# Four ends of stages in a two-layer graph kernel: products, row turns, first loads and batch statistics placed elsewhere

## The chip, the cores and the metric

The kernel runs on one NeuronCore of a Trainium2 chip. The metric is the device time of one execution in microseconds (us). The engines are PE (TensorE; PEld is its weight load), DVE (VectorE), ACT (ScalarE), POOL (GpSimd, which issues the gathers) and SP (SyncE, which issues the other DMAs).

## The reference, cut to what matters

```python
x = layernorm(x + L0(x))          # L0: GCN, two gcn_conv (128 -> 256 -> relu -> 128)
x = layernorm(x + L1(x))          # L1: attention messages, GRU, batch norm
# gcn_conv: h = x @ W; agg = segment_sum(h[src] * norm, dst) + h * dinv**2 + b
# L1, with 50000 nodes and 25000 edges sorted by dst:
att = sigmoid(xs @ W_att[:d] + xd @ W_att[d:] + b_att)        # xs = x[src], xd = x[dst]
aggregated = segment_sum((xs @ W_msg + b_msg) * att, dst)
gi = aggregated @ W_ih.T + b_ih;  gh = x @ W_hh.T + b_hh
r = sigmoid(i_r + h_r);  z = sigmoid(i_z + h_z);  n = tanh(i_n + r * h_n)
h_new = (1 - z) * n + z * x
return gamma * (h_new - mean(h_new, 0)) * rsqrt(var(h_new, 0) + eps) + beta
```

## The kernel before

The 50000 nodes are cut into NG = 98 groups of 512. After a preparation the kernel runs five passes over the groups, `scale`, `conv`, `norm`, `gru` and `final`. Each engine has its own program; in each pass it runs a function of the pass's name once per step, and `group_of(lag)` in it is the group that entered `lag` steps ago, so a step works on several groups, each at another phase. `run_pass` writes the first and the last steps out and makes loops of the rest. For `norm` the loops are unrolled by 8. Every order on an engine is that in which the code is written. Semaphores named by pass (`a_` conv, `n_` norm, `c_` gru, `o_` final) count finished groups.

The input may be irregular; a flag `slow_i`, worked out at the start, says so. PE, DVE and ACT have a FAST and a SLOW version of the passes with gathers, in two `If` blocks behind each other; the input here takes FAST. `both_ways` writes the two blocks. POOL issues three indirect gathers for each group in `conv`, `norm` and `gru` (`gathers`, L695), into four buffers `gath`.

- **conv** makes `G` (the rows that `norm` gathers, written by SP at L568) and `OWN` (the rows' own part, L570). Both DMAs of a group count on the same semaphore `a_st`. POOL starts `norm`'s gathers once all of `a_st` is in (`conv_rows_stored`).
- **norm**, on PE: the group's sum from the gathered rows (L1396, lag 0), its transposition (L1404, lag 4), the recurrent product of the candidate gate, `whh_sb[:, 2D:3D]` times the turned rows (L1410, lag 6), and the two attention columns (L1413, lag 6). DVE adds `OWN` (L1141, lag 2), makes the one-hot tiles (L1145, lag 0), copies the attention columns (L1153, L1154, lag 8; they release SP's store of `MT`, L589), and takes the row statistics (L1167 and the small ones after, lag 2 and 3). ACT takes the root (L810), scales (L816, lag 3), moves the turned rows out (L824, lag 5) and the recurrent product (L830, lag 7).
- **Between norm and gru**: outside the `If`, PE turns the collected attention columns `AD_ALL` (4 transpositions, L1420), ACT moves the result to `n_r[0]` (L835), SP stores it as `AD` (four DMAs, L597), and waits for all stores (`general_clear`). POOL starts gathering `MT` as soon as the stores of `YT` and `MT` are in.
- **gru**: SP loads for each group a row of `AD` to all partitions (`c_ad`, L611), at lag 2 the turned rows `YT` (`c_y`, L617) and, for 44 groups, `HN` (L620). The load of the attention row of groups 1, 2, 3 waits until ACT has finished the attention sigmoid (L868, `c_sgs`) of the group before it. DVE makes weighted one-hots (L1208), PE sums (L1445, lag 1) and, at lag 3, makes five products of 128x512: L1431 and L1437 from `whh_sb` and `c_y` for the gates r and z, L1433, L1435 and L1438 from the sum. On ACT L847 to L876 are the gates and a square with its sum over nodes; on DVE L1217 to L1237.
- **Behind gru**, outside the `If`: DVE reduces the sums (L1244 to L1249), ACT takes one root (L886, which needs another activation table, a load of its own at the same line), DVE makes factor and offset (L1251 to L1254), and **final** begins: POOL applies them (L741), PE transposes (L1465), DVE and ACT do the second row norm.

```python
            both_ways(norm, 6, unroll=8)          # PE, before
            pe.wait_ge(n_mc, NG)
            pe.wait_ge(n_trc, NG)
            for q, rows in enumerate(AD_CHUNKS):
                last = nc.tensor.transpose(bank[3][0:rows, q * P:(q + 1) * P], AD_ALL[:, q * P:q * P + rows], ident[:])
            last.then_inc(n_adt, 1)
            pe.wait_ge(n_hk, NG)
```

## Time and profile before

| | |
|---|---|
| median of 3 runs | 1756.09 us (1754.35 to 1758.73) |
| the profiled execution | 1759.59 us |
| its span in the trace | 1757.5 us |
| busy share of the span | PE 84%, DVE 80%, ACT 68%, POOL 60% |
| DMA moved | 433.97 MB, mean 247 GB/s |

The span runs from the first to the last instruction. The passes stand in it at about 189 to 626 us (conv), 631 to 1034 us (norm), 1045 to 1569 us (gru) and 1569 to 1757 us (final). Between two passes there is a seam in which most engines stand still: they can be seen in the page as low digits of PE's row.

### The profile page before, as it was taken

How to read it: one execution, taken by the hardware profiler on the slowest of the kernel's cores; microseconds unless marked ns; L12 is line 12 of the kernel's file. 1: busy time of each engine (PE TensorE's matmuls, PEld its weight loads, DVE VectorE, ACT ScalarE, POOL GpSimd, SP SyncE). 2: the span in 40 equal slices, each digit the busy share in tenths (PEclk: the TensorE clock that was granted, in tenths of full speed). 3: DMA queues.
4: the chain of work that ended last, by engine and by line, in shares of the span. 5: the costliest groups of instructions: out<-in, count | busy, mean ns of one | idle time of the engine just before them, and what ended most of it. 6: DMA issues, size and time to landing. Idle time of an engine off the chain costs nothing.

```text
span 1757.5 us, 35422 instructions
## 1 busy us (share of the span) xinstructions
PE 1473.8 (84%) x7678; PEld 1042.8 (59%) x7678; DVE 1398.1 (80%) x4668; ACT 1196.8 (68%) x3010; POOL 1053.4 (60%) x1014
## 2 busy tenths in 40 slices
PE   6300699999999958899999959999999999976765
PEld 3200477777777747778787845555555555545554
DVE  7817699999999858888888826888888888877786
ACT  6786355555555527777776746777777777757898
POOL 5000677777777547777777735666666666614442
PEclk9755799999999979999999979999999999988898
DMA  8798799998888738898776747777754444439998
GB/s 262 264 342 308 241 328 331 329 317 271 270 269 270 262 118 274 298 313 300 250 235 224 242 152 222 233 226 232 228 167 130 127 128 127 132 99 384 374 324 277
DMA packets 246942, 433.97 MB, mean 247 GB/s; under 512 B 41831, under 2 KB 44108, under 8 KB 246848
## 3 DMA queue, kind: packets, MB, share of 16 engines
q1 hardware_dynamic: 218160, 393.40, 65.8%
q0 software_dynamic: 28688, 39.54, 9.4%
q8 instruction: 31, 0.51, 0.1%
q14 instruction: 63, 0.52, 0.1%
HBM read 274.13 MB, written 178.01 MB: 257 GB/s over the span
## 4 chain that ended last, share of the span: by engine, by line
PE 61%; POOL 11%; DMA 11%; issue 6%; DVE 6%; ACT 4%; SPq 1%; DVEq 0%; ACTq 0%; POOLq 0%
POOL gath L695 10%; PE bank L1379 10%; PE bank L1371 10%; PE bank L1363 5%; PE bank L1431 5%; PE bank L1433 5%; PE bank L1445 5%; PE bank L1435 5%; PE bank L1438 5%; PE bank L1437 5%; DMA page<-YT 3%; PE bank L1396 3%; DMA gath<-G,ROWI 3%; ACT page L901 2%; DMA page<-in_x 2%
## 5 line engine op out<-in xcount | busy, mean ns | idle before, releaser
L695 POOL DMA_INDIRECT gath<-MT,ROWI x294 | 325.1, 1106 | 199.7 <-PE bank L1445 115.6
L695 POOL DMA_INDIRECT gath<-XP,ROWI x294 | 332.1, 1130 | 171.7 <-issue 88.7
L695 POOL DMA_INDIRECT gath<-G,ROWI x294 | 294.4, 1001 | 116.9 <-issue 83.8
L791 ACT ACTIVATE page<-bank,b_sb 128x512 f32<-128x512 f32 x196 | 124.0, 684 | 152.7 <-PE bank L1371 152.7
L1379 PEld LDWEIGHTS bank<-w_sb,page 128*128 128x128 f32 x1568 | 190.3, 192 | 46.4 <-issue 46.4
L1396 PE MATMUL bank<-gath,onehot 128*128 128x128 f32 x1176 | 161.0, 288 | 47.3 <-DMA gath<-G,ROWI 44.7
L1379 PE MATMUL bank<-w_sb,page 128*128 128x128 f32 x1568 | 190.7, 275 | 0.0
L1371 PE MATMUL bank<-page,w_sb 128*128 128x512 f32 x392 | 185.8, 597 | 0.0
L1363 PE MATMUL bank<-onehot,gath 128*128 128x170 f32 (+1 forms) x588 | 104.1, 314 | 94.9 <-DMA gath<-XP,ROWI 94.9
L1396 PEld LDWEIGHTS bank<-gath,onehot 128*128 128x128 f32 x1176 | 144.3, 198 | 51.2 <-issue 39.0
L1465 PE MATMUL bank<-ident,page 128*128 128x128 f32 x784 | 119.0, 304 | 62.2 <-DMA page<-YT 57.2
L816 ACT ACTIVATE page<-page,st_m,st_r 128x128 f32<-128x128 f32 x392 | 160.1, 479 | 0.0
L901 ACT ACTIVATE page<-bank,p_m,p_r 128x128 f32<-128x128 f32 x392 | 144.3, 497 | 22.2 <-DVE p_m L1287 13.1
L799 ACT ACTIVATE page<-bank,DINV 128x128 f32<-128x128 f32 x392 | 111.7, 368 | 58.5 <-PE bank L1379 57.9
L1465 PEld LDWEIGHTS bank<-ident,page 128*128 128x128 f32 x784 | 96.6, 155 | 85.2 <-issue 45.3
L1363 PEld LDWEIGHTS bank<-onehot,gath 128*128 128x128 f32 x588 | 88.9, 195 | 96.9 <-issue 94.5
L1413 PEld LDWEIGHTS bank<-watt_sb,page 128*128 128x128 f32 x784 | 103.6, 192 | 47.8 <-issue 47.3
L1445 PEld LDWEIGHTS bank<-onehot,gath 128*128 128x128 f32 x588 | 95.6, 193 | 59.7 <-issue 45.9
L861 ACT ACTIVATE page<-bank,brz_sb 128x512 f32<-128x512 f32 x98 | 67.3, 687 | 80.6 <-PE bank L1433 80.6
L1208 DVE SCALAR_TENSOR_TENSOR onehot<-iota_b,LOC,page 128x170 f32<-128x170 f32 (+1 forms) x294 | 98.9, 391 | 22.8 <-ACT page L868 22.5
L1120 DVE SCALAR_TENSOR_TENSOR page<-page,DINV 128x128 f32<-128x128 f32 x392 | 110.6, 341 | 5.9 <-issue 5.9
L868 ACT ACTIVATE page<-page,gath 128x170 f32<-128x170 f32 (+1 forms) x294 | 106.0, 426 | 13.3 <-DMA page<-AD 13.3
(224 smaller groups left out, 3292.7 us busy)
## 6 DMA issues: line engine op xcount, KB each, us to landing
page<-YT SPq DMA_DIRECT2D x196, 256.0 KB, 3.4
MT<-page SPq DMA_DIRECT2D x98, 260.0 KB, 3.3
XP<-page SPq DMA_DIRECT2D x98, 256.0 KB, 2.5
page<-in_xT SPq DMA_DIRECT2D x98, 256.0 KB
page<-DQ SPq DMA_DIRECT2D x98, 256.0 KB
G<-page SPq DMA_DIRECT2D x98, 256.0 KB
OWN<-page SPq DMA_DIRECT2D x98, 256.0 KB
page<-OWN SPq DMA_DIRECT2D x98, 256.0 KB
```

The lines of the kernel that those rows point to most:

```text
L695: nc.gpsimd.indirect_dma_start(gath[k][:, w, 0:width], None, rows, bass.IndirectOffsetOnAxis(ap=ROWI[:, at:at + 1], axis=0), bounds_check= ...
L791: last = nc.scalar.activation(rows[k], bank[2 + 2 * k + h][:], ACT.Relu, bias=b1_sb[:, h:h + 1])
L799: last = nc.scalar.activation(a_g[k][:, own], bank[6 + g.slot(2)][:, own], ACT.Copy, scale=DINV[:, bass.ds(g.index * J + j, 1)])
L816: last = nc.scalar.activation(n_m[g.slot(8)][:, j * DM:j * DM + D], n_z[k][:, j * D:(j + 1) * D], ACT.Identity, bias=st_m[k][:, j:j + 1], ...
L901: last = nc.scalar.activation(o_o[k][:, j * D:(j + 1) * D], bank[g.slot(8)][:, j * D:(j + 1) * D], ACT.Identity, bias=p_m[g.slot(8) // 2][ ...
L1120: last = nc.vector.scalar_tensor_tensor(a_r[k][:, own], a_g[k][:, own], DINV[:, bass.ds(g.index * J + j, 1)], a_xb[k][:, own], ALU.mult, A ...
L1363: last = nc.tensor.matmul(bank[k][:, at:at + n], gath[g.slot(4)][:, w, 0:D], onehot[k][:, at:at + n], start=True, stop=True)
L1371: last = nc.tensor.matmul(bank[2 + 2 * k + h][:], w1_sb[:, h * P:(h + 1) * P], a_T[k], start=True, stop=True)
L1379: last = nc.tensor.matmul(bank[6 + k][:, j * D:(j + 1) * D], rows[k][:, j * P:(j + 1) * P], w2_sb[:, h, :], start=(h == 0), stop=(h == 1))
L1396: last = nc.tensor.matmul(bank[k][:, j * D:(j + 1) * D], onehot[k][:, first:first + P], gath[g.slot(4)][:, w, 0:D], start=(i == 0), stop=( ...
L1445: last = nc.tensor.matmul(bank[k][:, at:at + n], gath[g.slot(4)][:, w, 0:D], onehot[k][:, at:at + n], start=True, stop=True)
L1465: last = nc.tensor.matmul(out_bank[:, tile], part[k][:, tile], ident[:], is_transpose=True, start=part is o_y and j == 0, stop=part is o_t ...
```

## The change

1. **Stores of conv**: the stores of `OWN` count on semaphores of their own (`own_st`, later used for the loads of `norm`). POOL waits for the stores of `G` alone before the first gather of `norm`. ACT and DVE wait, inside conv, each for its own kind.
2. **End of norm, PE**: the recurrent products of the last four groups (94 to 97) are taken out of the pass. Behind the last attention columns, still inside the `If`, PE makes those of groups 94 and 95, then the four transpositions of `AD_ALL`, then those of 96 and 97. ACT moves them out at matching places.
3. **norm, DVE**: the copy of the attention columns goes from lag 8 to lag 7, and from ahead of the row statistics to the end of the step. This holds in every step.
4. **Start of gru**: SP loads `c_y` of groups 0 and 1 ahead of the first attention row. PE makes their four products from `whh_sb` (r and z) before the first sum.
5. **End of gru**: the batch statistics on DVE and the root on ACT stand inside the `If` (in both versions), and ACT calls a root of a constant first, which brings its table in.

```diff
@@ gathers of norm, POOL
             def conv_rows_stored():
-                wait_all_dmas(pool, a_st, 2)
+                wait_all_dmas(pool, a_st)
                 pool.wait_ge(a_agg, NG)
@@ conv, SP
-                    sp.dma_start(group_of_table(OWN, g), a_r[k]).then_inc(a_st[k], 16)
+                    sp.dma_start(group_of_table(OWN, g), a_r[k]).then_inc(own_st[k], 16)
@@ gru, SP
+            for k in range(2):
+                sp.dma_start(c_y[k], YT[k:k + 1].rearrange("a p n -> (a p) n")).then_inc(c_iny[k], 16)
...
-                    sp.dma_start(c_y[k], group_of_table(YT, g)).then_inc(c_iny[k], 16)
+                    if not (g.fixed and g.index < 2):
+                        sp.dma_start(c_y[k], group_of_table(YT, g)).then_inc(c_iny[k], 16)
@@ norm, ACT
-            run_pass(act, norm, 7, unroll=8)
+            run_pass(act, norm, 6, unroll=8)
+            late = [Group(index // 8, index % 8, unroll=8) for index in range(LATE, NG)]
+            for g in late[:2]:
+                hidden(g)
             act.wait_ge(n_zz, NG)
             act.wait_ge(n_adt, 1)
             nc.scalar.activation(n_r[0], bank[3][:], ACT.Copy).then_inc(n_ad, 1)
+            for g in late[2:]:
+                hidden(g)
@@ gru, ACT
+            def batch_root():
+                nc.scalar.activation(p_q[0][:, 0:1], eps_sb[:, 0:1], ACT.Sqrt)
+                act.wait_ge(bn_v, 1)
+                nc.scalar.activation(bn[:, 3:4], bn[:, 2:3], ACT.Sqrt, bias=eps_sb[:, 1:2]).then_inc(bn_r, 1)
...
             with act.If(flag < 1):
                 run_pass(act, lambda group_of: gru(group_of, FAST), 5)
+                batch_root()
@@ norm, DVE
-                if g := group_of(8):
-                    k = g.slot(4)
...
+                normaliser(group_of(2), group_of(3), n_s6, n_sd, n_root, n_dq, n_var, n_rs)
+                if g := group_of(7):
...
-            both_ways(norm, 8, unroll=8)
+            both_ways(norm, 7, unroll=8)
@@ norm, PE
-                    wait(pe, n_hk, g.freed(2))
-                    nc.tensor.matmul(bank[6 + g.slot(2)][:], whh_sb[:, 2 * D:3 * D], y, start=True, stop=True).then_inc(n_hn, 1)
+                    if not (g.fixed and g.index >= LATE):
+                        recurrent(g)
...
+            def norm_end():
+                late = [Group(index // 8, index % 8, unroll=8) for index in range(LATE, NG)]
+                pe.wait_ge(n_trc, NG)
+                for g in late[:2]:
+                    recurrent(g)
+                pe.wait_ge(n_mc, NG)
+                for q, rows in enumerate(AD_CHUNKS):
+                    last = nc.tensor.transpose(bank[3][0:rows, q * P:(q + 1) * P], AD_ALL[:, q * P:q * P + rows], ident[:])
+                last.then_inc(n_adt, 1)
+                for g in late[2:]:
+                    recurrent(g)
@@ gru, PE
+                if g and g.fixed and g.index == 0 and mode is FAST:
+                    pe.wait_ge(n_ad, 1)
+                    for k in range(2):
+                        pe.wait_ge(c_iny[k], 16)
+                        nc.tensor.matmul(bank_r[k][:], whh_sb[:, 0:D], c_y[k], start=True, stop=False)
+                        nc.tensor.matmul(bank_z[k][:], whh_sb[:, D:2 * D], c_y[k], start=True, stop=False)
```

At the end of `norm` PE's row of instructions was this (before; `ident,DSQ` are the transpositions of the collected columns, `page,whh_sb` a recurrent product, `watt_sb,page` attention columns):

```order
L1404 MATMUL bank<-ident,page 128x128 x4
L1410 MATMUL bank<-page,whh_sb 128x512
L1413 MATMUL bank<-watt_sb,page 128x2 x4
L1410 MATMUL bank<-page,whh_sb 128x512
L1413 MATMUL bank<-watt_sb,page 128x2 x4
L1410 MATMUL bank<-page,whh_sb 128x512
L1413 MATMUL bank<-watt_sb,page 128x2 x4
L1351 UNCONDITIONAL_BRANCH
```

And now, in the lines of the changed file (L1445 transposes a group, L1426 is the recurrent product, L1454 the attention columns, L1464 turns the collected ones):

```order
L1445 MATMUL bank<-ident,page 128x128 x4
L1454 MATMUL bank<-watt_sb,page 128x2 x12
L1426 MATMUL bank<-page,whh_sb 128x512 x2
L1464 MATMUL bank<-ident,DSQ 128x128 x3
L1464 MATMUL bank<-ident,DSQ 8x128
L1426 MATMUL bank<-page,whh_sb 128x512 x2
L1386 UNCONDITIONAL_BRANCH
L1389 COMPARE_AND_BRANCH
```

The products went behind the columns, and the turning came inside the branch.

One step of `norm` on DVE, last written-out step ahead of the loop, before:

```order
L1141 TENSOR_TENSOR page<-bank,page 128x512
L1145 TENSOR_SCALAR onehot<-iota_b,LOC,WD 128x256 x3
L1153 COPY DSQ<-bank 128x4
L1154 TENSOR_TENSOR page<-bank,batt_sb 128x4x2
L1167 BN_STATS st<-page 128x6 x4
L1176 RECIPROCAL st_r<-st_q 128x4
```

and now (L1193 is the row statistics, L1184 and L1185 copy the attention columns):

```order
L1168 TENSOR_TENSOR page<-bank,page 128x512
L1172 TENSOR_SCALAR onehot<-iota_b,LOC,WD 128x256 x3
L1193 BN_STATS st<-page 128x6 x4
L1202 RECIPROCAL st_r<-st_q 128x4
L1203 SCALAR_TENSOR_TENSOR st_m<-st_s,st_q 128x4
L1208 TENSOR_TENSOR st_d<-st 128x4
L1209 TENSOR_TENSOR st_s<-st 128x4
L1210 TENSOR_TENSOR st_v<-st 128x4
L1212 TENSOR_TENSOR st_d<-st_d 128x4
L1216 TENSOR_TENSOR st_m<-st_m,st_r 128x4
L1220 SCALAR_TENSOR_TENSOR st_v<-st_d,st_v 128x4
L1184 COPY DSQ<-bank 128x4
```

The copy, which waits for PE's attention columns, is now the last thing of a step and stands ahead of the next step's addition.

The start of `gru` on PE, before (L1445 is the sum, L1431 and L1437 the products from `whh_sb`):

```order
L1445 MATMUL bank<-onehot,gath 128x172
L1445 MATMUL bank<-onehot,gath 128x170 x2
L1431 MATMUL bank<-page,whh_sb 128x512
L1433 MATMUL bank<-page,wc_sb 128x512
L1435 MATMUL bank<-page,wc_sb 128x512
L1437 MATMUL bank<-page,whh_sb 128x512
L1438 MATMUL bank<-page,wc_sb 128x512
```

and now (L1479 and L1480 are the four early products, L1503 the sum, L1490, L1492 and L1496 the rest of a group):

```order
L1479 MATMUL bank<-page,whh_sb 128x512
L1480 MATMUL bank<-page,whh_sb 128x512
L1479 MATMUL bank<-page,whh_sb 128x512
L1480 MATMUL bank<-page,whh_sb 128x512
L1503 MATMUL bank<-onehot,gath 128x172
L1503 MATMUL bank<-onehot,gath 128x170 x2
L1503 MATMUL bank<-onehot,gath 128x172
L1503 MATMUL bank<-onehot,gath 128x170 x2
L1490 MATMUL bank<-page,wc_sb 128x512
L1492 MATMUL bank<-page,wc_sb 128x512
L1496 MATMUL bank<-page,wc_sb 128x512
```

Two products of each of the first two groups now stand ahead of every sum.

## Rows read from the trace of the kernel before

**Rows 1.** Busy time by stretch: PE, PEld, DVE, ACT, POOL, then PEclk, DMA share, GB/s

```profile
700.00:760.00 60.00, 55.02 (x403) 47.48 (x403) 51.48 (x282) 43.49 (x108) 45.93 (x47) 1.00 0.92 307
940.00:1000.00 60.00, 57.29 (x398) 49.01 (x398) 50.17 (x271) 42.20 (x106) 45.99 (x47) 0.94 0.70 228
1180.00:1240.00 60.00, 60.00 (x185) 31.90 (x184) 50.63 (x106) 47.10 (x105) 38.80 (x36) 1.00 0.74 231
```

**Rows 2.** Chain that ended last, seam between conv and norm: start us, us, what

```profile
626.61 3.83 DMA OWN<-page
630.46 0.74 issue
631.20 0.99 POOL gath L695
```

**Rows 3.** Timeline there, SP's queue: start us, us, engine line op out<-in [idle before <-releaser]

```profile
625.38 0.33 SPq L568 DMA_DIRECT2D G<-page  x1
```

**Rows 4.** Timeline inside norm, one step of DVE and PE

```profile
902.70 0.69 DVE L1141 TENSOR_TENSOR page<-bank,page 128x512 f32<-128x512 f32 x1
...
903.55 0.95 PE L1413 MATMUL bank<-watt_sb,page 128*128 128x2 f32 x8
...
904.65 0.16 DVE L1153 COPY DSQ<-bank 128x4 f32 x1 [0.26 <-PE bank L1413]
...
906.32 0.69 DVE L1141 TENSOR_TENSOR page<-bank,page 128x512 f32<-128x512 f32 x1
```

**Rows 5.** Timeline, last steps of norm, DVE and ACT

```profile
1021.32 0.16 DVE L1153 COPY DSQ<-bank 128x4 f32<-128x4 f32 x1 [1.25 <-PE bank L1413]
...
1025.68 1.64 ACT L816 ACTIVATE page<-page,st_m,st_r 128x128 f32<-128x128 f32 x4
```

**Rows 6.** Chain that ended last, from norm's last products to gru's first load

```profile
1032.06 0.96 PE bank L1410 x2
1033.02 0.80 PE bank L1413 x8
...
1034.09 1.85 issue
1035.94 0.87 PE bank L1420 x3
1036.82 2.37 issue
...
1044.89 3.30 DMA page<-AD
```

**Rows 7.** Timeline, first steps of gru, ACT and PE

```profile
1048.21 1.09 ACT L868 ACTIVATE page<-page,gath 128x172 f32<-128x172 f32 x3 [6.44 <-DMA page<-AD]
...
1052.53 1.09 ACT L868 ACTIVATE page<-page,gath 128x172 f32<-128x172 f32 x3 [3.22 <-DMA page<-AD]
...
1058.30 2.07 PE L1431 MATMUL bank<-page,whh_sb 128*128 128x512 f32 x2 [1.51 <-DMA page<-YT]
...
1063.03 1.09 ACT L868 ACTIVATE page<-page,gath 128x172 f32<-128x172 f32 x3 [0.23 <-DMA page<-AD]
...
1075.14 1.03 PE L1445 MATMUL bank<-onehot,gath 128*128 128x172 f32 x6
```

**Rows 8.** One line's DMAs (L617, `page<-YT`), 1040 to 1075 us: landing

```profile
DMA to landing us min/median/max: 2.8/4.7/5.9
```

**Rows 9.** Timeline, end of gru, ACT and DVE

```profile
1569.13 0.19 ACT L876 ACTIVATION_READ_ACCUMULATOR page<-keep 128x1 f32 x1
...
1570.98 0.26 DVE L1244 TENSOR_REDUCE bn<-hsum 128x1 f32<-128x98 f32 x1 [2.28 <-issue]
...
1571.36 1.28 ACT L886 ACT_TABLE_LOAD   x1 [2.04 <-issue]
```

**Rows 10.** Timeline, end of norm, ACT's earlier change of table, and the copy ahead of it

```profile
1039.66 0.60 ACT L835 ACTIVATE page<-bank 128x512 f32<-128x512 f32 x1 [6.00 <-PE bank L1420]
1040.28 1.28 ACT L836 ACT_TABLE_LOAD   x1
```

More of the change, by code:

```diff
@@ L52 @@
 BACK = max(at - P * w for w, (at, n) in enumerate(FAST_COLS))
+LATE = NG - 4
 AD_CHUNKS = [min(P, NT - at) for at in range(0, NT, P)]
@@ L1255, in _ @@
+            flag = dve.value_load(slow_i[0:1, 0:1], min_val=0, max_val=1)
+            chained = count[0]
+            with dve.If(flag < 1):
+                run_pass(dve, lambda group_of: gru(group_of, FAST), 4)
+                batch_map()
+            count[0] = chained
+            with dve.If(flag > 0):
+                run_pass(dve, lambda group_of: gru(group_of, SLOW), 4)
+                batch_map()
             wait_all_dmas(dve, h_st, 2, FREE)
@@ L1346, in _, with both_ways @@
             general_tensor(pe, 0, D)
-            def both_ways(step, lag, unroll=U):
+            def both_ways(step, lag, unroll=U, end=lambda: None):
                 flag = pe.value_load(slow_i[0:1, 0:1], min_val=0, max_val=1)
@@ L1385, in _, with recurrent @@
             general_tensor(pe, 1, D)
+            def recurrent(g):
+                wait(pe, n_hk, g.freed(2))
+                nc.tensor.matmul(bank[6 + g.slot(2)][:], whh_sb[:, 2 * D:3 * D], n_T[g.slot(4)], start=True, stop=True).then_inc(n_hn, 1)
             def norm(group_of, mode):
@@ L1414, in norm @@
                     last.then_inc(n_mm, 1)
-            both_ways(norm, 6, unroll=8)
-            pe.wait_ge(n_mc, NG)
-            pe.wait_ge(n_trc, NG)
-            for q, rows in enumerate(AD_CHUNKS):
-                last = nc.tensor.transpose(bank[3][0:rows, q * P:(q + 1) * P], AD_ALL[:, q * P:q * P + rows], ident[:])
-            last.then_inc(n_adt, 1)
+            def norm_end():
[9 more added lines that the diff above has]
+                    recurrent(g)
+            both_ways(norm, 6, unroll=8, end=norm_end)
             pe.wait_ge(n_hk, NG)
```

83 lines of the change are left out of this document (48 added, 35 removed).

## The prediction

> **What bounds the kernel now.** I read the busy time by stretch first, then the chain of work that ended last, then the timeline at each seam. In `norm` POOL is the bound: 46 or 47 gathers in 60 us, 45.93 to 45.99 us busy, and each gather is followed by 0.30 us of its own issue, so that 46 of them fill the 60 us at 1.30 each [rows 1]. A group costs 3 x 1.30 = 3.9 us. PE has 55 to 57 of 60 us there and DVE 50 to 51, so both keep slack, PE little. In `gru` PE is busy 60.00 of 60 us: it is the bound, and a group takes 5.16 us (16 matmuls a group, 185 in 60 us) [rows 1]. What is won inside these passes on DVE, ACT or SP is worth nothing; what is won at a seam moves the whole rest. So I price the seams, and ask of every edit inside a pass whether it could make a new bound.
>
> **Seam conv to norm.** POOL's first gather at 631.20 follows the landing of the last store of `OWN`, issued at 626.61 and landed 3.83 us later [rows 2]. The last store of `G` was issued at 625.38 [rows 3]. With the same landing time it is in 1.23 us earlier, and the 0.74 us of issue behind it stays. POOL is the bound up to the last gather, so this passes on to the end of the pass: **-1.2 us**. It can't be below 0, since the new wait is a part of the old one, and little above. ACT, DVE and SP now wait for eight semaphores rather than four; this is hidden, since the first one-hot is needed only when three gathers have landed, some 5 us after the first. Inside conv the split waits free nobody: the chain runs through PE there.
>
> **Norm on DVE.** The copy L1153 waits for PE's attention columns. In a steady step the next addition L1141 started at 902.70, before PE's columns of that step (903.55 to 904.50), and DVE waited 0.26 us for them at 904.65; the next step began at 906.32 [rows 4]. So DVE works 3.62 - 0.26 = 3.36 us in a step. Now the columns come first: the addition starts about 2 us later against PE. Behind the waiting copy are queued the addition (0.7 us), on which PE's sum two steps on waits, and the one-hots (1.1 us). PE's sum needs them one PE step later, which is 3.5 us, and they are there after 0.2 + 0.7 + 1.1 = 2.0. DVE's own 3.36 stays under 3.9. Price in the steady part 0; there POOL's buffers cover it (four groups deep). The bound on the other side is a rival below.
>
> **End of norm.** Here PE is the chain. In the last steps a group costs one recurrent product of 0.96 and columns of 0.80 us [rows 6]. Taking out the four products removes 3 x 0.96 = 2.9 us from the path; the fourth (group 94) I count at nothing, because PE would then wait for the last transposition, which needs ACT's scaling at 1025.68 [rows 5]. The moved copy costs a bit: DVE's copy at 1021.32, which had waited 1.25 us, now stands ahead of the addition of group 97, which had run during that wait, so that statistics come 0.7 us later [rows 5]. Most of this fits into slack on ACT; I count +0.2. Sum so far -2.7.
>
> From the end of the last columns (1033.82) to the end of the turning (just ahead of ACT's copy at 1039.66 [rows 10]) the chain had 5.8 us: DVE's copy, 1.85 us of issue, three transpositions 0.87, 2.37 of issue, the fourth [rows 6]. Now two products come first, 2 x 0.96 = 1.9, and cover DVE's copy; then four transpositions in straight code, 0.87 + 0.4, and 0.1 for semaphores: 3.3. That is -2.5, and the term **-5.2 us**. Between ends: if the 2.37 returns at some point of the new piece, -2.8; if all goes smoother, -5.9. The two remaining products lie behind the turning and beside ACT's copy and SP's stores. `MT`'s last store goes 2.7 us earlier, so the gathers do as well; they were not last before.
>
> The two idle times of 1.85 and 2.37 us in which PE waited for nothing shown stand right behind the end of the `If` [rows 6]; I take them to be the cost of leaving it. The Trainium skill, Runtime: NRT & Kernel Launch, Instruction fetch mechanics, says that a taken branch whose target is not at hand makes the engine fetch by DMA first, and that straight code is fetched ahead. By that rule PE still pays behind its last products, where SP's stores (over 5 us to the next load at 1044.89) cover it.
>
> **Start of gru.** Count from S, SP's first load (1044.89). Before: first attention sigmoid at S+3.3, the second at S+7.6, the fourth at S+18.1, PE's first product only at S+13.4, at half clock (two matmuls in 2.07 us), and the fifth sum at S+30.3 (1075.14); from there PE runs without a gap [rows 7]. The attention rows climb a ladder, since each load waits for the sigmoid before: 14.8 us for three rungs. Now two `YT` loads stand ahead of the first row. Two issues cost about 0.8 us; and a row lands in 3.3 us alone [rows 6], while loads in a crowd took 2.8 to 5.9, median 4.7 [rows 8]. I take 4.3, nearer the crowd's median: the first sigmoid at S+5.1, 1.8 later than before (between 0.7 and 3.4). The rungs lose two `YT` loads as company; I take 4.75 each, between the quickest rung of 4.32 and the mean of 4.94 [rows 7]: the fourth sigmoid at S+19.4. The four early products (3.4 us at full clock, 8.3 at 2.07 each) run from about S+4; the first sum may be late by 2 to 3 us, but the second waits for the second rung anyway. Behind the ladder PE no longer has ten products for two groups to make up but six, so it keeps pace, and what is late next is the ladder plus one round of ACT and DVE: 1.1 for the sigmoid, 2.2 for ACT's other gates (4.1 us a group less sigmoid and square), 4.4 for DVE's group [rows 1]. The fifth sum comes at 19.4 + 1.1 + 2.2 + 4.4 = S+27.1 instead of S+30.3: **-3.1 us** (from -1.5 to -4.2 by the delay of the first row; 0 if PE is late too).
>
> **End of gru.** ACT's last square ended at 1569.32; DVE's first reduction came at 1570.98, ACT's table load at 1571.36 after 2.04 us of idle time, and the root behind it at 1572.64 [rows 9]. Now the load starts at 1569.35 and ends at 1570.63, the root of the constant takes 0.2, and DVE's reductions, 1.2 us from 1569.4, are done by then: root at 1570.9. **-1.8 us**. The way out of the `If` now lies behind the factor, where ACT and DVE wait for PE's first turned rows. The final pass has to load its table again (1.28), hidden in the same wait.
>
> A table load took 1.28 us and began 0.02 us after an activation [rows 10]. The Trainium skill, ScalarE: Activation LUTs, What ACT_TABLE_LOAD costs, adds a drain of some 1380 ns to every switch. That would be a result of its own: the last term would shrink to -0.4 and the time rise by 1.4. The row speaks against it, and I go by the row.
>
> **Sum.** 1.2 + 5.2 + 3.1 + 1.8 = 11.3 us. Against the profiled execution 1759.59 this is 1748.3. That execution lay 3.5 us above the median of the runs shown (1756.09), so I forecast 1744.8. The lows of the terms, 0 + 2.8 + 0 + 0.4, give 3.2 (1752.9); the highs, 1.3 + 5.9 + 4.2 + 1.9, give 13.3 (1742.8), and two medians of runs may differ by 2 us.
>
> **Rivals.**
> - *The front of gru gives nothing*: attention rows behind two loads of 256 KB, or the early products at half clock in the way of the first sums. For: rows 8 allow a delay of 3.4. Against: PE has nothing else to do until the first attention sigmoid, over 8 us behind its last transposition [rows 7, 10]. Sum 8.2, 1747.9. Chance 0.13.
> - *The issue gap returns* in the new end of norm (1747.2), alone 0.08, together with the rival above (1750.3) 0.06; *the drain is real* (1746.2) 0.03.
> - *The seams don't add up*: the gains don't pass on, because DMA-bound stretches (92% in norm's first half [rows 1]) or the final pass take them back; 1753 or so, 0.07.
> - *Slower*: the copy at the end of a DVE step ties DVE to PE. If waits for the columns, the addition and PE's sum closed a loop longer than POOL's 3.9 us, each 0.1 us would cost 9.6 us over some 96 groups. It decides against us from 4.02 us on; at 4.1 the time is 1744.8 + 19 = 1764. For: PE has only 3 to 5 us of slack in 60. Against: the 1.5 us of room worked out above, and buffers four deep. 0.05.
> - *Forecast*: 0.58.
>
> **Chances.** A measurement can tell about 0.3% from no change, so faster means below 1750.8. Faster 0.82, within 0.3% 0.13, slower 0.05. Range for 8 in 10: 1740.5 to 1753.
>
> **What would show it.** The first gather of norm about 1.2 us nearer the last sum of conv; gathers still 1.30 us apart through norm; no idle time above 0.5 us between PE's last columns and the end of the turning; the first attention sigmoid 5 us behind SP's first load of gru, and the fifth sum at 27; the table load directly behind the last square. It is wrong if PE waits for DVE inside norm, if a gap of 2 us stands between the transpositions, or if the fifth sum still comes 30 us behind the first load.

## The result

The changed kernel took 1754.61 us, median of 12 runs, beside 1759.15 us for the kernel before in the same comparison: a ratio of 0.9976 with a 95% interval of 0.9965 to 0.9986. The forecast was 1744.8, with a range up to 1753.0, so the measured time lies outside it. The difference is 4.5 us where 11.3 were forecast. Some 3 us of the miss in the absolute time come from the three runs of before that the forecast started from (1756.09); the rest is a gain that isn't there. The ratios leave out slow executions, here one of the changed kernel (2337.71 us at a mean granted clock of 0.64) and two of the kernel before (1910.51 and 2346.03 us). Three later comparisons of the same two kernels gave 0.9986, 0.9984 and 0.9979, so that the four together stand at 0.998, or some 3.4 us. The sign was right; by the bound of 0.3% the change makes no difference.

The profiled execution has a span of 1752.3 us, against 1757.5 before. In the seam between conv and norm the chain of work that ended last (start us, us, what) now follows the last store of `G`:

```profile
626.40 4.14 DMA G<-page
630.54 0.03 POOLq L728
630.57 0.74 issue
631.31 1.00 POOL gath L705
```

From that store's issue to the first gather 4.91 us went by, where 5.82 had (625.38 to 631.20, [rows 2, 3]). The last sum of norm then started at 1017.5 us here and 1017.6 before, since the last store of `G` itself had gone out 1.0 us later (626.40 against 625.38). The same chain at the end of norm reads quite unlike [rows 6]:

```profile
1028.58 1.09 PE bank L1445 x4
1029.67 4.91 PE bank L1454 x24
1034.58 3.62 PE bank L1426 x4
1038.20 0.74 PE bank L1464 x4
```

The 24 matmuls of three groups' attention columns (L1454) took 4.91 us, 1.64 a group, where a group's had taken 0.80. Two recurrent products (L1426, four matmuls) took 3.62, 1.81 each, where they had taken 0.96. The turning itself (L1464) has lost both idle times of 1.85 and 2.37 us. The reason for the slow products is in PE's windows (from:to, length, PE busy and count, granted clock, DMA share, GB/s):

```profile
1026.00:1028.00 2.00, 1.42 (x12) 1.00 0.65 250
1028.00:1030.00 2.00, 1.42 (x8) 0.60 0.43 159
1030.00:1034.00 4.00, 4.00 (x20) 0.50 0.87 330
1034.00:1038.00 4.00, 4.00 (x8) 0.50 0.36 135
```

The granted clock fell from 1.00 (2.4 GHz) to 0.50 (1.2 GHz) within the second of two pieces in which PE was busy 1.42 of 2 us. Most of the idle time in them is one wait of 1.09 us, until ACT had moved turned rows out (L835), where before PE had a recurrent product to do:

```profile
1028.58 1.09 PE L1445 MATMUL bank<-ident,page 128*128 128x128 f32 x4 [1.09 <-ACT page L835]
```

In the kernel before, the same rows of windows read:

```profile
1030.00:1032.00 2.00, 1.87 (x15) 1.00 0.43 162
1032.00:1034.00 2.00, 2.00 (x12) 1.00 1.02 383
1034.00:1036.00 2.00, 2.00 (x13) 1.00 0.94 355
```

(These are from a second profile of before, in which everything from norm on lies some 3 us later; it is the kernel e12 below.)

At the start of gru, PE's timeline (start us, us, engine, line, operation, [idle before <-releaser]) shows the early products L1479 and L1480 behind the two loads, and the fifth sum at 1072.21 instead of 1075.14 [rows 7]:

```profile
1048.09 2.04 PE L1479 MATMUL bank<-page,whh_sb 128*128 128x512 f32 x2 [7.45 <-DMA page<-YT]
1049.93 1.91 PE L1480 MATMUL bank<-page,whh_sb 128*128 128x512 f32 x2
...
1056.31 1.14 PE L1503 MATMUL bank<-onehot,gath 128*128 128x172 f32 x6 [1.58 <-DVE onehot L1234]
...
1072.21 1.11 PE L1503 MATMUL bank<-onehot,gath 128*128 128x172 f32 x6 [0.27 <-issue]
```

At the end of gru the chain no longer passes through the batch factor. It goes from ACT's last square to SP and to a load of the final pass:

```profile
1565.88 0.58 ACT page L896 x2
1566.46 0.02 issue
...
1566.55 0.33 SPq L646
...
1567.87 4.98 DMA page<-YT
```

### The profile page after: what moved, and what is told of

The parts are those of the page before. It is cut to its first block, busy times and chain, and to the rows that moved or that the text cites. A ratio compares the mean times of both kernels' runs of the same rounds, so it can differ in the third digit from the quotient of the medians.

```text
span 1752.3 us, 35433 instructions
## 1 busy us (share of the span) xinstructions
PE 1476.5 (84%) x7678; PEld 1042.4 (59%) x7678; DVE 1394.2 (80%) x4668; ACT 1197.3 (68%) x3012; POOL 1057.6 (60%) x1014
## 4 chain that ended last, share of the span: by engine, by line
PE 56%; POOL 16%; DMA 10%; issue 7%; ACT 4%; DVE 4%; SPq 1%; DVEq 0%; ACTq 0%; POOLq 0%
POOL gath L705 16%; PE bank L1416 10%; PE bank L1408 9%; PE bank L1503 5%; PE bank L1490 5%; PE bank L1488 5%; PE bank L1496 5%; PE bank L1492 5%; PE bank L1495 5%; PE bank L1400 5%; DMA page<-YT 3%; ACT page L927 2%; DMA page<-in_x 2%; DMA XP<-page 1%; PE bank L1523 1%
## 5 line engine op out<-in xcount | busy, mean ns | idle before, releaser
L705 POOL DMA_INDIRECT gath<-XP,ROWI x294 | 336.1, 1143 | 172.8 <-issue 84.1
L1437 PE MATMUL bank<-gath,onehot 128*128 128x128 f32 x1176 | 161.0, 288 | 45.0 <-DMA gath<-G,ROWI 43.4
L1437 PEld LDWEIGHTS bank<-gath,onehot 128*128 128x128 f32 x1176 | 144.0, 197 | 49.4 <-issue 34.6
L1454 PEld LDWEIGHTS bank<-watt_sb,page 128*128 128x128 f32 x784 | 105.8, 197 | 46.0 <-issue 46.0
L1503 PEld LDWEIGHTS bank<-onehot,gath 128*128 128x128 f32 x588 | 93.9, 190 | 52.3 <-issue 48.4
L821 ACT ACTIVATE st_q<-st_v,eps_sb 128x4 f32<-128x4 f32 x98 | 29.1, 297 | 130.6 <-DVE st_v L1220 128.9
```

The lines of the kernel that those rows point to most:

```text
L705: nc.gpsimd.indirect_dma_start(gath[k][:, w, 0:width], None, rows, bass.IndirectOffsetOnAxis(ap=ROWI[:, at:at + 1], axis=0), bounds_check= ...
L1437: last = nc.tensor.matmul(bank[k][:, j * D:(j + 1) * D], onehot[k][:, first:first + P], gath[g.slot(4)][:, w, 0:D], start=(i == 0), stop=( ...
L1503: last = nc.tensor.matmul(bank[k][:, at:at + n], gath[g.slot(4)][:, w, 0:D], onehot[k][:, at:at + n], start=True, stop=True)
```

## The experiments

**How they are compared.** From each profile I read the same marks: the start of norm's last sum, the end of the attention columns, the end of the turning, and the start of gru's fifth sum, from which PE is busy without a longer gap. The table gives them in us after the last sum's start, by the timelines, and the ratio of times to the kernel before with its interval. (By the chain the sum starts 0.13 us later; the expectations of the first runs count the changed kernel's 21.41 from there, as 21.28.) "Late" is the number of recurrent products taken out of the pass; "order" is the place of DVE's attention copies (old: lag 8, ahead of the statistics; new: lag 7, behind them).

| kernel | late | order | turning in branch | columns | turning | fifth sum | ratio |
|---|---|---|---|---|---|---|---|
| before | 0 | old | no | 16.20 | 21.95 | 57.53 | |
| e12 (before again) | 0 | old | no | 16.20 | 21.95 | 57.52 | |
| e16 seam only * | 0 | old | no | 16.20 | 22.14 | 58.17 | 0.9993 (0.9984 to 1.0002) |
| e8 batch statistics only * | 0 | old | no | 17.30 | 22.77 | 59.71 | 0.9996 (0.9982 to 1.0009) |
| e11 late only | 4 | old | no | 16.33 | 20.75 | 56.61 | 0.9982 (0.9972 to 0.9991) |
| e9 turning only | 0 | old | yes | 16.21 | 17.19 | 54.73 | 0.9981 (0.9969 to 0.9994) |
| changed kernel | 4 | new | yes | 17.06 | 21.41 | 54.69 | 0.9976 (0.9965 to 0.9986) |
| e6 (changed again) * | 4 | new | yes | 15.80 | 19.85 | 52.77 | 0.9986 (0.9972 to 1.0000) |
| e13 (changed again) * | 4 | new | yes | 15.93 | 20.04 | 53.88 | 0.9984 (0.9974 to 0.9994) |
| e18 (changed again) * | 4 | new | yes | 16.83 | 21.30 | 55.42 | 0.9979 (0.9966 to 0.9992) |
| e2 old order | 4 | old | yes | 13.97 | 18.45 | 50.53 | |
| e14 (e2 again, timed) * | 4 | old | yes | 17.24 | 21.55 | 55.54 | 0.9973 (0.9962 to 0.9984) |
| e4 changed, with filler | 4 | new | yes | 14.25 | 17.59 | 51.48 | 0.9956 (0.9939 to 0.9973) |
| e1 no late | 0 | new | yes | 16.92 | 17.97 | 51.73 | 0.9941 (0.9926 to 0.9956) |
| e10 no late, old order | 0 | old | yes | 16.20 | 17.24 | 50.60 | 0.9954 (0.9937 to 0.9970) |
| e17 (e10 again) * | 0 | old | yes | 17.14 | 18.19 | 54.68 | 0.9966 (0.9953 to 0.9979) |
| e3 two late | 2 | new | yes | 15.21 | 16.25 | 49.06 | 0.9939 (0.9925 to 0.9952) |
| e15 (e3 again) * | 2 | new | yes | 15.41 | 16.46 | 52.75 | 0.9972 (0.9962 to 0.9982) |
| e5 two late, old order * | 2 | old | yes | 15.72 | 17.23 | 52.52 | 0.9958 (0.9941 to 0.9974) |
| e7 as e5, no gru front * | 2 | old | yes | 15.33 | 16.84 | 54.87 | 0.9960 (0.9944 to 0.9976) |

The rows with a star ran on three other chips (e5 to e8, e13 to e16, e17 and e18), on which the kernel before takes 1852 to 1865 us instead of 1759 to 1761. Norm takes 452 to 462 us there from first gather to last sum, and 386 to 388 elsewhere. Times are compared with the kernel before on the same chip only.

**e1, no late product.**

```
-LATE = NG - 4
+LATE = NG
-            run_pass(act, norm, 6, unroll=8)
+            run_pass(act, norm, 7, unroll=8)
```

> The changed kernel with the four last recurrent products back in the pass; the turning of the attention rows stays inside the branch, and the rest of the change stays. Theory A: taking the products out of the drain leaves TensorE idle, its granted clock falls to half, and the attention columns then cost 1.64 us a group instead of 0.79. Then here the granted clock stays at 1.00 to the end of the columns; last sum's start to the end of the columns 16.1 to 16.7 us (changed kernel 16.92, before 16.07), turning done 1.3 to 2.5 us later, so 17.6 to 18.8 in all against 21.28 and 21.83: a span 2.5 to 3.7 us shorter than the changed kernel's, 1748.6 to 1749.8. Theory B (the two vector copies, issued ahead of the statistics, make the last groups late and TensorE idle for them): the clock still falls near the end, 20 to 21.3 us in all, span 1751 to 1752.5. Theory C (the products do cost their 0.96 us each, and the fall of the clock belongs to the end of the stage whatever is issued): 21.3 us or more, span at least 1752.

Measured: 17.97 us to the end of the turning, a ratio of 0.9941, span 1750.2 (0.4 above what theory A had given it; the columns ended 0.1 us later than it had). The clock was at 1.00 to the end of the columns. All four products are back in PE's way, and the stretch is 3.4 us shorter than in the changed kernel's first profile. PE's timeline shows columns at 0.8 us a group to the end, and the turning 0.42 us behind them:

```profile
1033.81 1.10 PE L1426 MATMUL bank<-page,whh_sb 128*128 128x512 f32 x2
1034.75 0.95 PE L1454 MATMUL bank<-watt_sb,page 128*128 128x2 f32 x8
1036.12 0.63 PE L1464 MATMUL bank<-ident,DSQ 128*128 128x128 f32 x4 [0.42 <-DVE page L1185]
```

**e2, the old vector order, four late.** The two copies stand ahead of the statistics again, as at lines 1149 to 1154 of the kernel before.

> The changed kernel with VectorE's pair of attention copies back behind the statistics' place of before (lag 8, ahead of them); the four products stay late. Theory A: TensorE still idles in the drain where the products stood, the granted clock still falls to half, and last sum's start to the end of the turning stays within 0.7 us of the changed kernel's 21.28 us. Theory B: the statistics of the last group start 0.65 us earlier, the two idle stretches of 0.67 and 1.14 us before the last sums go, the clock stays at 1.00, and the same stretch takes 16.5 to 17.5 us. Theory C: as A.

Measured, in one execution of 1753.82 us beside 1760.09: 18.45 us, with the clock at half from 13 us after the last sum on. Most of the columns had run at the full clock by then, and they ended at 13.97. The stretch is 3 us shorter than the changed kernel's, which spoke for theory B in part. It was timed again later (e14), and that took it back.

**e3, two late products, both behind the turning.**

```
-LATE = NG - 4
+LATE = NG - 2
-                for g in late[:2]:
+                for g in late[:0]:
...
-                for g in late[2:]:
+                for g in late:
```

> The changed kernel with only the last two recurrent products taken out of the pass, and both put behind the turning. Theory A: the products of groups 94 and 95 keep TensorE at work, as far as they stand between the last sums the clock stays at 1.00 (or falls late, after most of the columns); last sum's start to the end of the turning 15.2 to 17 us against 21.28: a span 4 to 6 us shorter than the changed kernel's, 1746.3 to 1748.3, the fastest of these. Theory B: the last groups are late as before, the clock falls with them, 20 to 21.3 us, span 1751 to 1752.3. Theory C: only the products' place counts, 19.4 to 21.3 us, span 1750.4 to 1752.3.

Measured: 16.25 us, the shortest of all, and a ratio of 0.9939. The clock stayed at 1.00 until behind the turning; three groups' columns took 2.59 us in the chain, as against 4.91. The profiled span, 1753.2, is above the 1746.3 to 1748.3 expected; it belongs to the slowest of its five executions (1755.29; the others lie at 1748.3 to 1751.2), and the excess lies in the final pass.

**e4, more work.** The changed kernel with one product that nobody reads, ahead of each of the last two groups' transpositions:

```
+                    if g.fixed and g.index >= NG - 2:
+                        wait(pe, n_zz, NG - 1)
+                        nc.tensor.matmul(bank[0][:], whh_sb[:, 2 * D:3 * D], keep[:, 0:GN], start=True, stop=True)
                     wait(pe, n_yy, g.done())
```

> The changed kernel with work added: TensorE multiplies whh_sb by 512 columns of keep into bank 0, once ahead of each of the last two groups' transpositions, and nothing reads the result (the outputs stay what they were). Each costs about one product, 0.96 us at the full clock. Theory A: more work, less time: TensorE stays busy where it idled, the granted clock stays at 1.00 into the columns, and last sum's start to the end of the turning falls below the changed kernel's 21.28 us, to 16.5 to 19. Theories B and C: the added products cost 0 to 1.9 us, 21.3 to 23.2 us, span 1752.3 to 1754.2.

Measured: 17.59 us, ratio 0.9956. PE's timeline shows the fillers (L1444) and behind them three groups' columns (L1457) in 2.74 us, and its windows the full clock under them:

```profile
1029.62 1.10 PE L1444 MATMUL bank<-keep,whh_sb 128*128 128x512 f32 x2
1030.67 0.63 PE L1448 MATMUL bank<-ident,page 128*128 128x128 f32 x4
1031.13 2.74 PE L1457 MATMUL bank<-watt_sb,page 128*128 128x2 f32 x24
1033.73 2.62 PE L1426 MATMUL bank<-page,whh_sb 128*128 128x512 f32 x4
1036.15 1.06 PE L1467 MATMUL bank<-ident,DSQ 128*128 128x128 f32 x4
```

```profile
1030.00:1032.00 2.00, 2.00 (x15) 1.00 0.43 160
1032.00:1034.00 2.00, 2.00 (x18) 1.00 1.02 384
```

Work was added, the order of everything else was kept, and the stretch became 2.3 to 3.8 us shorter than in the four profiles of the changed kernel (19.85 to 21.41). The rivals allowed no gain from it. The idle time of 1.1 us is gone with it. This is the experiment on which theory A rests.

**e6, the changed kernel again, and e5, both causes out.** e5 is e3 with DVE's old order.

> The changed kernel once more, as the yardstick of this batch and to see which differences between stages come back. If the clock's fall belongs to the order of this kernel (theory A), the granted clock is again at half before the last attention columns, and last sum's start to the end of the turning is again 21.4 us within 0.5 (changed kernel 21.41, with the last sum at 1017.52 and the turning's end at 1038.93). If it was a matter of one execution, the stretch comes out near 17 us. From the end of the batch factors to the end of the span, 183.1 to 187.8 us in the profiles so far with the same code, another value in that band is expected; the median within 2 us of 1754.6.

> Two late products, both behind the turning, and VectorE's attention copies at their old place (lag 8, ahead of the statistics): both causes of idle TensorE in the drain taken out together. The copies' new order cost 2.96 us while four products were late (21.41 with it, 18.45 without). If it costs by its own, last sum's start to the end of the turning falls from 16.25 us (two late, new order) to 14.5 to 15.8; if it only cost through the fallen clock, it stays at 16.0 to 16.6, since the clock was full there. The median 0 to 1.5 us below that of the kernel with two late products and the new order (1750.5), and 4 to 6 us below the changed kernel's.

Measured for e6: the clock at half again, from 12.5 us after the last sum on instead of 11, and 19.85 us, outside the 21.4 within 0.5 that were expected. When the clock falls differs from one execution to the next, that it falls does not. For e5: 17.23 us, not 14.5 to 15.8, with the clock falling during the last group's columns. Its time was 8.0 us below the kernel before and 6.9 below e6.

**e7, no front of gru.** e5 without the two early loads and the four early products.

> The kernel with two late products and the old order of the vector copies, less the front of gru: no early loads of the first two groups' rows, no early products. If that part is worth what the two traces showed (end of the turning to the fifth sum 35.58 us before, 33.28 after, 32.1 to 33.9 in the other kernels that have it), the stretch comes out 35 to 36 us and the median 2 to 3 us above that of the same kernel with it. Rival: most of the gain in that stretch is the arrival of the other loads, which start earlier by themselves; then the stretch stays under 34 us.

Measured: 38.03 us from the end of the turning to the fifth sum, against 35.29 with that part on the same chip: 2.7 us, near the 3.1 of the prediction, though both lie above what was expected (35 to 36, and 32.1 to 33.9). The medians don't show it (1844.5 and 1844.3, where 2 to 3 us were expected), with intervals of some 3 us each; whether it arrives at the end stays open.

**e8, the batch statistics alone.**

> The kernel before with one part of the change alone: the batch statistics inside the branch, with the square root's table loaded ahead. If the part adds to the others undiminished, fifth sum to the last batch factor is 496.56 us against 498.42 (-1.86), and the median is 1 to 2.5 us below that of the kernel before. Rival: the last pass is held by its transfers, which start with this factor in neither kernel, and the gain comes back there: then the factor is as early, the stretch behind it longer by 1.9 us, and the median within 0.7 us of the kernel before.

Measured: 0.9996, nearest the rival's case, though the interval reaches to 3 us of gain. ACT's table load and DVE's reductions stand directly behind the last square, as in the changed kernel:

```profile
1663.65 0.19 ACT L876 ACTIVATION_READ_ACCUMULATOR page<-keep 128x1 f32 x1
1663.86 1.28 ACT L882 ACT_TABLE_LOAD   x1
1663.87 0.25 DVE L1248 TENSOR_REDUCE bn<-hsum 128x1 f32<-128x98 f32 x1 [0.64 <-ACT page L876]
1663.93 0.33 SPq L636 DMA_DIRECT2D page<-HT  x1
...
1666.15 0.16 DVE L1258 TENSOR_TENSOR bn<-gb_sb,bn 128x1 f32<-128x1 f32 x1
...
1666.81 0.77 POOL L741 TENSOR_SCALAR page<-page,bn 128x512 f32<-128x512 f32 x1 [32.49 <-DMA page<-HT]
...
1667.39 1.94 PE L1479 MATMUL bank<-ident,page 128*128 128x128 f32 x8 [8.08 <-DMA page<-YT]
```

The factor is there, and POOL's first scaling now waits for a load of `HT`; PE waits for one of `YT`. SP issues the first of them right behind the last square (0.47 us to the first `YT` load, in all 20 profiles). From the end of the last square to the end of the span the five profiles without this part took 186.5 to 188.4 us (mean 187.6), the fifteen with it 185.2 to 190.1 (mean 187.3). That is a difference of 0.3 us where the factor is 1.9 earlier; with single profiles that lie up to 5 us apart it is known to within some 1 us.

Where the gain goes can be seen in the same 20 profiles. POOL's first scaling moves from 4.5 to 4.7 us behind the last square to 2.9 to 3.1. Its second stands at 5.3 to 6.1 without the part and at 4.3 to 5.8 with it, and its tenth at 19.3 and 19.4 in the mean. PE's first transposition, at 3.6 to 4.1 and 3.5 to 3.7, waited for its load of `YT` in both kernels.

**e9, the turning alone.** The kernel before with its four transpositions moved inside the branch (`norm_end`).

> The kernel before with one part alone: the turning of the attention rows inside the branch. The prediction takes 2.5 us for it (1.85 and 2.37 us of idle time given to instruction issue, less what has to be waited for). Then last sum's start to the end of the turning is 19.0 to 19.8 us, as against 21.95. Theory C, which gives this part all that the drain can gain: 17.5 to 18.6 us. Rival: the idle time comes back inside the branch, 21 to 22 us, and then it wasn't the branch's end.

> The kernel before once more, for a profile on this chip. Expected from the stage's own work: the granted clock at 1.00 through the attention columns, last sum's start to the end of the turning 21.9 us within 1, the end of the turning to the fifth sum 35.6 within 2, the fifth sum to the last batch factor 498.4, and from there to the end of the span 183 to 188.

Measured: 17.19 against 21.95 in both profiles of before: 4.8 us, twice the 2.5 of the prediction, and beyond what theory C had given it. e12 came out as expected. Both idle times are gone: PE's four transpositions come 0.33 us behind DVE's copy. But at the fifth sum only 2.8 us of it are left (54.73 against 57.53), since the chain has another late one:

```profile
1036.54 4.58 DMA MT<-page
...
1041.49 0.75 issue
...
1042.24 1.00 POOL gath L695
```

The last store of `MT` goes out 16.5 us after the last sum, right behind DVE's last columns, and takes 4.58 us. Before (e12), the chain at this place was

```profile
1043.72 0.43 SPq L597
...
1044.19 1.33 SPq L597
...
1045.57 2.17 DMA AD<-page
...
1048.06 3.63 DMA page<-AD
```

and POOL's gathers began 20.2 us after the last sum; now they begin 22.2 us after it (from 1020.03), and ACT's first two sigmoids of gru wait for a gather instead of a row of `AD`.

**e11, the late products alone.** The kernel before with the four products taken out, two at the branch's end, two behind the turning, which stays outside.

> The kernel before with one part alone: the four last recurrent products taken out of the pass, two ahead of the branch's end and two behind the turning, which stays outside the branch; VectorE's order as before. The prediction took 2.7 us for it. Theory A: the granted clock falls to half within the last attention columns, as in the changed kernel with the vector order of before (18.45 us there with the turning inside the branch); last sum's start to the end of the columns 13.5 to 16 us instead of 16.20, and to the end of the turning 20.5 to 23.5, so a gain under 1.5 us, or a loss. By the prediction's term: columns done at 13.5, turning done at 19.2 to 19.5.

Measured: columns done at 16.33, not 13.5, and 0.3 us above theory A's range too. The clock fell where it does in the changed kernel (10.3 us after the last sum, 10.9 there), and the same two groups of the chain took the same time:

```profile
1028.61 1.09 PE bank L1422 x4
1029.70 4.91 PE bank L1431 x24
1034.61 3.62 PE bank L1403 x4
```

One part of the change alone, DVE in its old order, and the same 4.91. The end of the turning comes 1.2 us earlier than before, since two products now lie behind it and the two ahead of it stand in place of an idle time.

**e10, none late and the old order; e17 and e18, once more beside each other.**

> The changed kernel with no late product and VectorE's copies at their old place: of the end of norm only the turning inside the branch is left of the change. If the turning alone carries the gain there, last sum's start to the end of the turning is 17.3 to 18.2 us (17.97 with the new vector order), and the median within 1.5 us of that of the kernel with two late products and the old order (8.0 us below the kernel before, in its own batch). If the two late products are worth their 0.96 us each, it is 1 to 2 us above that.

> No late product, VectorE's copies at their old place, all the rest of the change. Stage by stage as before: last sum's start to the end of the columns 16.20 us, to the end of the turning 17.24, both at the full granted clock. Its gain in time over the changed kernel: 2 to 4 us if the late products cost what the stages show (17.24 against 19.85 to 21.41 at the end of norm), about 7 if the larger of the two earlier differences was right, under 1.5 if the smaller one was.

> The changed kernel beside it. The granted clock at half before the last attention columns, last sum's start to the end of the turning 19.8 to 21.5 us; 0.9975 to 0.9985 of the kernel before.

Measured: e10 had its columns done at 16.20 and the turning at 17.24, just below what was expected of the turning alone, and was 8.2 us below the kernel before. e17, the same kernel on another chip, had 17.14 and 18.19, a miss, so that the 0.7 us between e1 and e10 can't be put down to DVE's order either. In time e17 was 1.7 us below e18, under the 2 to 4 expected and within the noise of both. e18 itself came out as expected.

**e13 to e16, timed on one chip.** e13, e14 and e15 are the changed kernel, e2 and e3; e16 is the kernel before with the separate semaphore for `OWN` alone.

> The changed kernel, timed beside its three variants. Expected: the clock at half before the last attention columns, last sum's start to the end of the turning 19.8 to 21.5 us, and the slowest of this batch but for the kernel with the seam alone: about 0.9975 of the kernel before.

> The changed kernel with VectorE's copies at their old place, four products late, now timed. Its profile had 18.45 us at the end of norm against 21.41, and the fifth sum of gru 4.2 us earlier after the last sum of norm. If the vector order costs that much while four products are late, the median is 2 to 4.5 us below the changed kernel's; if the one profile misled, it is within 1 us.

> Two late products, both behind the turning, with the new vector order, beside the changed kernel on one chip. Theory A, the products that fill the drain keep the clock: end of norm 16 to 17.5 us, the fifth sum of gru 4 to 5.6 us earlier after the last sum of norm than in the changed kernel, and the median 3.5 to 5.5 us below its. Rival, the gain at norm is given back at the gathers of gru, which wait for the last stores of MT: a median less than 2.5 us below.

> The kernel before with one part alone: the own rows' stores on a semaphore of their own, so that the first gathers of norm wait for the G stores only. By the prediction, last G store's issue to the first gather 4.6 us instead of 5.82 (changed kernel 4.91), and the time 0.9 to 1.2 us below the kernel before, which the measurement can hardly tell from nothing. Rival: the OWN stores' landing isn't the late one on most executions, and nothing moves: 5.6 to 6 us.

Measured: e13 came out as expected. e14 came out at 21.55 us with the clock falling early, and 1.1 us below e13 in time. So the old order doesn't guard the clock: e2's 18.45 was an execution in which it fell late. Theory B is out. e15 kept 16.46 at the end of norm, 3.6 us less than e13, but only 1.1 of them at the fifth sum, and 0.9 in time: its rival's figures, but not its reason. ACT's first sigmoid waited for a row of `AD`, not for a gather, and the fourth sum still came 2.8 us earlier than in e13 (45.4 us against 48.2); from there to the fifth 7.3 us went by instead of 5.7. e16 had 5.01 us from the last `G` store to the first gather, between the 4.6 expected and its rival's 5.6 to 6. The five profiles that wait for both tables have 5.05 to 5.82 (mean 5.5), the fifteen others 3.46 to 5.13 (mean 4.7). That is 0.8 us, with a time too near to no change to tell.

## Why the prediction failed, point by point

- **Seam conv to norm, -1.2.** Right in kind, 0.9 in the two traces and 0.8 over twenty profiles. The landing of `G` was taken as equal to that of `OWN`, 3.83; it took 4.14.
- **Norm on DVE, 0.** Held: from the first gather to the last sum 386.2 us against 386.4. The slower rival, a copy that ties DVE to PE, is refuted.
- **End of norm, -5.2: the step that failed.** It was 0.5 us in the traces compared, and 1.3 with the mean of the changed kernel's four profiles, 20.65, against 21.95. "Taking out the four products removes 3 x 0.96 from the path" priced the removed work at the full clock, and the rest at the clock that the removed work had kept up. In all seven profiles with four late products and no filler, in either order of DVE and with the turning in or out of the branch, PE had an idle time of 1.1 us in the drain, which none of the others had, and the granted clock went to half before the columns were done. In all eight with none late it was at 1.00 up to their end. Two late products or two fillers kept it up through most or all of the columns. In e2, where it fell latest, the columns ended at 13.97, near the 13.5 that the term asked for: the subtraction was right for as long as the clock stayed up. With the products gone and the early fall, the columns alone gave it all back (16.33 in e11 against 16.20). None of the rivals had this.
- **The turning, -2.5 of those.** Mis-sized in the other direction: alone it took 4.8 us off the stretch (e9). With it and no late product (e10) the end of norm reaches 17.24, close to the 16.75 that the whole term asked for. The idle times of 1.85 and 2.37 us [rows 6] did belong to the branch's end, as argued; the rival in which one returns is refuted.
- **The copy order, +0.2.** Not to be told from the spread. The columns end between 13.97 and 17.24 with four late products, whichever order.
- **"They were not last before."** The prediction let `MT`'s last store and the gathers go 2.7 us earlier. In the four profiles of the changed kernel the store went out 16.1 to 17.4 us behind the last sum, against 16.5 before, since the columns were hardly earlier, and the gathers began at 20.0 to 21.2 us against 20.2; ACT's first sigmoid waited for a row of `AD` there, as before. The gathers became the late ones where the rows were turned early (e1, e3, e5, e7, e9 and e10); in e9, e10 and e1 they began at 22.2 to 22.9. In e9 this takes back some 2 of the 4.8 us.
- **Start of gru, -3.1.** 2.6 in the traces (30.3 to 27.7 us behind the first load), 2.7 by e7. The ladder came as forecast: the first sigmoid 5.0 us behind the first load and the fourth 19.7, where 5.1 and 19.4 were worked out. The first two of the four early products did run at half clock, as allowed for. The rival that it gives nothing falls for the stage; for the whole time it is open.
- **End of gru, -1.8, "passes on".** The factor came 1.9 us earlier, from 498.4 to 496.6 us behind the fifth sum. No drain beside the table load: ACT's root began 1.41 us behind the load's start. The rule of the Trainium skill that spoke against the term (ScalarE: Activation LUTs, What ACT_TABLE_LOAD costs) isn't what failed; the trace doesn't show that drain. What failed is "passes on". SP's loads of the final pass start right behind the last square in both kernels. The factor was the late one for POOL's first scaling alone, by some 1.5 us; PE's first transposition, and POOL from its third scaling on, waited for loads before as after. The twenty profiles put the gain of the part at 0.3 of 1.9. The rival "The seams don't add up", with a chance of 0.07, had named the final pass as a place that takes gains back.

Put together: 0.8 + 1.3 + 2.6 + 0.3 makes 5.0 us, near the 3.4 to 4.5 measured. (By the table, the changed kernel's fifth sum comes 3.3 us earlier in the mean of four, less than 1.3 + 2.6, which makes it 4.4.) Of the 6.3 us that are missing from 11.3, the end of norm has 3.9, the end of gru 1.5, and the two others 0.9.

**A better version.** Every variant of the changed kernel with fewer late products had a lower ratio than the changed kernel: e1 (0.9941) and e3 (0.9939) beside e10 (0.9954), with e17 and e15 at 0.9966 and 0.9972 on chips with a longer norm, where their intervals overlap those of the changed kernel beside them. The mean of the six ratios with fewer late products and the turning inside (e1, e3, e5, e10, e15, e17) is 0.9955, that of the changed kernel's four 0.9981. Which of none and two is the better one the intervals don't tell. How much of it arrives differs by batch, by 0.9 to 6.9 us against the changed kernel beside it; of what this depends on, only the start of gru is seen (e15 and e17: 52.75 and 54.68 us at the fifth sum with norm ending at 16.46 and 18.19). In e5, e15 and e17 the step from the fourth sum to the fifth took 7.3 to 8.4 us, in the changed kernel 5.7. What holds it there stays open.

## What to carry to other kernels

Removing work that PE does while it waits for another engine isn't a sure gain: it may hold the clock for the short products around it, so look at the granted clock of the stretch before a product is priced out of a drain, and price what stays at both levels. A term at a seam counts only up to the next wait; before a gain is summed, read which transfer or store lands second there, since a stage whose loads start on an event of their own takes back what is won beside them. The single profile that showed 3 us for one order of DVE was an accident of when the clock fell, and a second one showed none.

## What the runs showed of the hardware that was not expected

- The clock fell with PE busy 1.42 of each 2 us, behind one idle time of 1.1 us, among matmuls of 2 and of 128 columns. In all seven such profiles it fell 0.9 to 3.7 us after that idle time began. Behind an idle time of 0.6 us alone (e1 and e3) it stayed up to the end of the columns. In e4 the clock fell later, at 15.3 us, with no idle time above 0.2 us, behind the 24 matmuls of two columns; so what the idle time and what the short matmuls do to it isn't told apart. In the seven it came back to 1.00 only 7 to 10 us after the fall, behind the products of 512 columns at half speed.
- Leaving the `If` of PE cost two idle times, of 1.85 us at once and 2.37 us three instructions further on; both went when the four transpositions were moved inside (4.8 us in e9). The profile of before has four transfers of instructions there, two from 1033 to 1036 us and two from 1036 to 1039.2; in e9 there is none from 1030 us to the end of the turning at 1037.2. Which engine they were for it doesn't say. That agrees in kind with the Trainium skill, Runtime: NRT & Kernel Launch, Instruction fetch mechanics, where a taken branch whose target is not at hand has to wait for a fetch.
- The same program takes 1759 to 1761 us on some chips and 1852 to 1865 on others, with stages of much the same length from the end of norm on (494.2 to 494.8 us from the fifth sum to the last square, in all 20 profiles). The difference is in conv and above all in norm, where POOL comes to 39 gathers in 60 us instead of 47. The group of the gathers between 700 and 760 us (busy us, mean ns of one | idle before it), in e6 and then in the changed kernel's first profile:

```profile
L705 POOL DMA_INDIRECT gath<-G,ROWI x39 | 38.9, 997 | 21.5 <-issue 9.2 <-remote 6.6 <-PE bank L1437 5.6
```

```profile
L705 POOL DMA_INDIRECT gath<-G,ROWI x47 | 47.1, 1002 | 14.3 <-issue 14.3
```

  A gather costs POOL the same; it waits more between them. What makes it wait there was not looked into.
